# A product of constants ahead of the first weights, and the centring of W moved up, in a GNN and mixture-of-experts kernel on one core

## The chip, the cores and the metric

The kernel runs on one core of a Trainium2 chip. The metric is the device time of one execution in microseconds. The kernel before took 1074.32 us, the median of three runs (1073.18 to 1074.93).

## The reference

x has 6250 rows of 256 columns, and there are 206250 edges, sorted by their target (100000 drawn ones in both directions, and one loop for each node). The kernel computes, with LN for a layer norm without gain:

```
deg  = number of edges that end at a node (+1 for the second loop)
h    = LN(x) @ W;  norm = 1/sqrt(deg[src] * deg[dst])
agg  = segment_sum(h[src] * norm, dst) + b;  x = x + prelu(agg)
z    = LN(x);  routing = softmax(mean(z) @ Wr + br), rescaled, top 2 of 8 experts
ffn  = sum over the 2 experts of weight * (gelu(z @ W1 + b1) @ W2 + b2)
out  = x + LN(z + ffn) * gamma + beta
```

Two parts of it matter here. The layer norm in front of W is not applied to x: since LN subtracts the mean of each row, the kernel subtracts from each column of W that column's mean instead (it **centres** W), multiplies the raw x with it, and scales afterwards. And the degrees are found from the sorted targets.

## The kernel before

The 6250 nodes are T = 49 blocks of P = 128. Each engine runs its own program, and the order is written out by hand with semaphores. The stages are a prologue (until about 85 us), the sums over the edges (until about 764 us), the routing (until about 778 us) and the expert layers. Only the prologue is touched.

**SyncE** issues the loads in this order: the targets of all edges (`dst_all`, L576 and L578), W (L579), then x in five parts (L581).

**GpSimd** writes the first constants at L678: `ident`, `eps`, `ones` (128x128 of 1.0) and the first column of W. Each raises the semaphore `first_consts`; a fifth count comes from L680, which finishes `ident`. L682 then makes `position`, and further constants follow.

**TensorE** waits for all five counts and for W, and sums W's columns over the partitions with two f32 products, `ones` times W (L1708, into bank 5). Then `turn_x` (L1718) transposes the two halves of a block of x, two blocks ahead, and `make_h` (L1728) multiplies the turned block with W in two f32 products. `tiles(lo, hi)` is a `make_h` and a `turn_x` for each block. After `tiles(0, 5)` comes the flag product (L1743 and L1744, into bank 7), which says whether the degree search found a plain case; it waits for `unsorted_ready` and `found` from VectorE. `tiles(5, 7)` follow, then seven steps of twelve bf16 count products (L1753), one tile between two of them. L1780 is the first product that needs the degrees.

**VectorE** works in program order. L878 makes `rise`, the differences of neighbouring targets. L880 makes `mark[1]` from the targets and `position`: it is the second operation of the **degree search**. L884 centres W, in two operations, once TensorE's column sums are there (`w_mean`). L888 needs `rise` and `mark[1]`; then come L891, twelve maxima of 136 columns (L896), and small operations up to L913, which raises `unsorted_ready`. L917 reads the flag. Then VectorE makes the one-hot matrices of the counts (L936, L923, L940).

**ScalarE** copies every turned block out of PSUM (L1503) and every product (L1508), and sums its squares (L1516).

Of the kernel before, what the change touches and what calls it, by code (L numbers as in the profile page):

```python
# [6 lines left out]
ALU = mybir.AluOpType  # L7
# [9 lines left out]
P = 128  # L17
# [36 lines left out]
def edge_columns(E):  # L54

    assert RANGE % (2 * SC) == 0
    return -(-(-(-E // P)) // RANGE) * RANGE
# [7 lines left out]
def gnn_ffn_kernel(nc, a, out, E):  # L65
    x, src, dst, pairs = a["x"], a["src"], a["dst"], a["pairs"]
    N, D = out.shape
    NX, _, F = a["W1"].shape
    T = -(-N // P)
    REST = N - (T - 1) * P  # L70
    KD, KF = D // P, F // P
    COLS = edge_columns(E)
# [10 lines left out]
    POS_BITS = SEG.bit_length()  # L83
# [16 lines left out]
    WARM = (9, 8, 4)  # L100
    CF = TOP_K * KF
    GF = 4
    EARLY_W1 = 2
    GATHERED = sorted(d for first in GFIRST for d in range(first, T - 3, GCYCLE))
    FROM = 2
# [21 lines left out]
    HALVES = [(h * HALF, h * HALF + ROWS, list(picks(DENSE[h::2], GCYCLE - 1))) for h in range(2)]  # L127
    LISTED = list(picks(GATHERED, 1))
    N_KEYS = sum(len(cols) for _, _, cols in HALVES)
    N_STARTS = N_KEYS + len(LISTED)  # L130
    TABLE_PARTS = ((0, 8), (HELD, 32), (8, 16), (32, 40), (16, HELD), (40, T))
# [30 lines left out]
    with ExitStack() as ctx:  # L162
        def sb(name, shape, dt=F32):
            return ctx.enter_context(nc.sbuf_tensor(name, shape, dt))

        def sem(name):
            return ctx.enter_context(nc.semaphore(name))
# [10 lines left out]
        ones = sb("ones", [P, P])  # L178
# [67 lines left out]
        REGION_END = TAB_AT + T * 2 * D * WORD  # L246
        W1_AT = ADJ_AT - EARLY_W1 * KD * F * WORD
        assert (NX - EARLY_W1) * KD * F <= P * T and LAST == 1
        RING_AT = ADJ_AT - RING * (2 * D + P) * WORD - 2 * GCH * 2 * WORD - 64
# [50 lines left out]
        dst_all = room("dst_all", [P, COLS + 1], I32)  # L300
# [4 lines left out]
        position = room("position", [P, COLS])  # L305
        mark = [room(f"mark{i}", [P, COLS]) for i in range(2)]
# [30 lines left out]
        gl = room("gl", [P, 2, CF, GT * P], F32R)  # L337
        assert 2 * CF * GT * P >= (NX - EARLY_W1) * KD * F
        W2e = room("W2e", [P, TOP_K, KF, D])
# [4 lines left out]
        gh = room("gh", [P, 2, CF, GT * P], F32R)  # L344
        gf = room("gf", [P, GF, GT * P])
        zb, x1b = (room(n, [P, 2, GT, D]) for n in ("zb", "x1b"))
# [12 lines left out]
        cum_ps, off_ps, flag_ps = banks[5], banks[6], banks[7]  # L359
# [12 lines left out]
        position_made = sem("position_made")  # L372
# [5 lines left out]
        first_consts = sem("first_consts")  # L378
# [109 lines left out]
        N_FIRST = 5  # L488
# [58 lines left out]
        def block_edges(eng, d):  # L547

            return (eng.value_load(table[0:1, 0, ds(d, 1)], min_val=0, max_val=EDGES),
                    eng.value_load(table[0:1, 1, ds(d, 1)], min_val=1, max_val=MAXB),  # L550
                    eng.value_load(table[0:1, 2, ds(d, 1)], min_val=0, max_val=MAXB * T))
# [121 lines left out]
        def _(pool):  # L673
# [47 lines left out]
            def load_W1(lo, hi):  # L721
                for e in range(lo, hi):
                    g.dma_start(W1a[:, e, :, :], a["W1"][e, :, :].rearrange("(k p) f -> p k f", p=P)).then_inc(w1_in, 16)
# [5 lines left out]
            with pool.If(is_dense(pool)):  # L729
# [44 lines left out]
                pool.wait_ge(row_used, NGATH * GCH)  # L774
                load_W1(0, EARLY_W1)
                for d in (2 * GT - 2, 2 * GT - 1):
# [3 lines left out]
                pool.wait_ge(acc_ready, T - 1)  # L780
                load_W1(EARLY_W1, NX)
            with pool.Else():
                tab_made(pool)
                for buf, pattern, m in ((gpos, [[RANGE, NRANGE]], COLS), (block_node, [[P, T]], 0), (batch_starts, [[BATCH, MAXB]], 0)):
                    g.iota(buf[:, :], pattern, base=0, channel_multiplier=m, allow_small_or_imprecise_dtypes=True).then_inc(g_consts, 1)

                pool.wait_ge(table_ready, 1)
                pool.wait_ge(h_stored, 16)
                def gathers(d):
                    load_tile(d, 0)  # L790
                    _, n, first = block_edges(pool, d)
                    with pool.Fori(0, n) as j:
                        b = first + j
                        for h, (lo, hi) in enumerate(PARTS):
                            pool.wait_ge(src_in[h], (b + 1) * 16)
                            for u in range(lo, hi):
                                hold(pool, slot_free, b * U + (u + 1))
                                g.indirect_dma_start(
                                    out=rows[:, u, :], out_offset=None, in_=h_table,
                                    in_offset=bass.IndirectOffsetOnAxis(ap=src_ix[h][:, u - lo:u - lo + 1], axis=0),  # L800
                                    bounds_check=T * P - 1).then_inc(rows_in[u], 16)
                    store_x1(d, 0)
                    finish_x1(0, d * 16 + 16)

                with pool.Fori(0, T) as d:
                    gathers(d)
                pool.wait_ge(acc_ready, T)
                pool.wait_ge(x1_out, T + 2)
                load_W1(0, NX)
                load_x1()  # L810
# [31 lines left out]
        def _(dve):  # L842
            v = nc.vector
            pro = [0]

            def step(ins):
                pro[0] += 1
                ins.then_inc(dve_pro, 1)

            def settled():  # L850
                dve.wait_ge(dve_pro, pro[0])
# [5 lines left out]
            dve.sem_inc(zl_kept, KD)  # L857
            dve.sem_inc(gl_made, GF)
            dve.sem_inc(norm, 2 * NORM)
# [10 lines left out]
            def x_variance(tiles):  # L870
                settled()
                for t in tiles:
# [3 lines left out]

            dve.wait_ge(edges_in, 32)
            v.tensor_tensor(rise[:, :], dst_all[:, 1:COLS + 1], dst_all[:, 0:COLS], ALU.subtract).then_inc(rise_made, 1)  # L878
            dve.wait_ge(position_made, 1)
            step(v.scalar_tensor_tensor(out=mark[1][:, :], in0=dst_all[:, 0:COLS], scalar=float(1 << POS_BITS), in1=position[:, :],  # L880
                                        op0=ALU.mult, op1=ALU.add))
            dve.wait_ge(w_mean, 1)
            for k in range(KD):
                v.scalar_tensor_tensor(out=W[:, k, 1:D + 1], in0=cum_ps[:, 0:D], scalar=-1.0 / D, in1=W[:, k, 1:D + 1],  # L884
                                       op0=ALU.mult, op1=ALU.add).then_inc(w_centred, 1)
            dve.wait_ge(rise_made, 1)
            settled()
            step(v.scalar_tensor_tensor(out=mark[0][:, :], in0=rise[:, :], scalar=0.0, in1=mark[1][:, :], op0=ALU.is_gt, op1=ALU.mult))  # L888
# [87 lines left out]
            def root_of(lo, hi):  # L976
# [13 lines left out]
                                   op0=ALU.mult, op1=ALU.add).then_inc(decoded, 1)  # L990
# [404 lines left out]
            def split_g(g, k, n, tiles=range(CF)):  # L1395
                for c in tiles:
                    dve.wait_ge(g_made, g * (2 * CF) + (2 * c + 10))
                    v.tensor_tensor(gl[:, k, c, 0:n], gf[:, c % GF, 0:n], gh[:, k, c, 0:n].bitcast(F32), ALU.subtract).then_inc(gl_made, 1)  # L1398

# [58 lines left out]
            for k in range(TOP_K):  # L1458
# [4 lines left out]
                                         op0=ALU.mult, op1=ALU.add))  # L1463
            assert rs[0] == ROUTE_B2
            split_g(0, 0, GT * P, range(2, CF))
            for k in range(TOP_K):
                dve.wait_ge(w_split, 2 * TOP_K + k + 1)
                rstep(v.scalar_tensor_tensor(out=W2l[:, k, :, :], in0=W2e[:, k, :, :], scalar=wts[:, k:k + 1],
                                             in1=W2h[:, k, :, :].bitcast(F32), op0=ALU.mult, op1=ALU.subtract))
# [18 lines left out]
        def _(act):  # L1488
# [164 lines left out]
            def gelus(g, k, n, tiles):  # L1653
                for c in tiles:
# [5 lines left out]
                    act.wait_ge(gl_made, g * CF + (c + 1))  # L1660
                    s.activation(gf[:, c % GF, 0:n], h1_ps[c % 4][:, 0:n], ACT.Gelu, bias=bias).then_inc(g_made, 1)  # L1661

# [34 lines left out]
        def _(pe):  # L1697
            mm = nc.tensor.matmul
# [3 lines left out]
            pe.sem_inc(edges_turned, 1)  # L1702
            pe.sem_inc(z_turned, 2)
            pe.sem_inc(y_made, 2 * GT)
            pe.wait_ge(first_consts, N_FIRST)
            pe.wait_ge(w_in, 16)
            for q in range(KD):
# [40 lines left out]
            with pe.If(by_runs(pe)):  # L1748
                for c in range(RSTEPS):
                    k = c % 2  # L1750
                    pe.wait_ge(ones_ready, c * 2 + 2)
                    for q in range(SC):
                        last = mm(deg[:, 0:T], hot_src[:, k, :, q], hot_run[k][:, q // PAIR, :, q % PAIR],  # L1753
                                  start=(c == 0 and q == 0), stop=True, skip_group_check=True)
# [174 lines left out]
            with pe.Else():  # L1929
# [14 lines left out]
                with pe.Fori(0, T) as d:  # L1944
                    _, n, first = block_edges(pe, d)
# [41 lines left out]
            def output(g, k, n, between=None):  # L1987
                pe.wait_ge(rt, ROUTE_END)
                pe.wait_ge(gl_made, g * CF + (CF + GF))
                for m in range(n):  # L1990
# [70 lines left out]
```

## Time and profile before

| | us |
|---|---|
| median of three runs | 1074.32 |
| the profiled execution | 1075.31 |
| its span, first to last instruction | 1073.8 |
| outside the span | 1.5 |
| TensorE busy in the span | 1048.2 |
| VectorE busy | 815.8 |
| ScalarE busy | 683.0 |
| GpSimd busy | 518.9 |
| TensorE's first matmul starts | 6.5 |

Times are microseconds from the start of the span. A matmul's recorded length holds its way through the array as well as its columns, so matmuls that follow each other overlap in the records; how fast they go is read from the chain of work, which cuts them to what each adds. An f32 product is two passes, and has two matmul records and two weight loads. The granted clock of TensorE is a share of 2.4 GHz: 1.00 is the upper level, 0.50 the lower (1.2 GHz).

### The profile page before, as it was taken

What the parts mean: (1) busy time and instruction counts of PE and PEld (TensorE: products, weight loads), DVE (VectorE), ACT (ScalarE), POOL (GpSimd) and SP (SyncE); (2) the same over time, 40 slices, a digit from 0 to 9 for tenths busy, and PEclk for the clock granted to TensorE, in tenths of its full rate; (3) what the DMA queues carried; (4) which work ended last, traced back from release to release, by engine and by line L of the source; (5) the groups of instructions that cost most, each with busy time, mean ns of one, the idle gap of its engine ahead of it and who ended that gap; (6) DMA issues with size and microseconds to landing.
All of it is one profiled execution on the core that took longest, in us unless ns stands there. A gap on an engine that the chain in (4) does not pass through costs nothing.

```text
span 1073.8 us, 20081 instructions
## 1 busy us (share of the span) xinstructions
PE 1048.2 (98%) x6264; PEld 892.4 (83%) x6267; DVE 815.8 (76%) x1947; ACT 683.0 (64%) x1511; POOL 518.9 (48%) x520
## 2 busy tenths in 40 slices
PE   6999999999999999999999999999899999999996
PEld 5787888888888888888888888888689999999995
DVE  6897777868686867776777777866477878878786
ACT  5794565767666676666666766675386474656551
POOL 4102566677767776777677767771201111111111
PEclk9999999999999999999999999999899999999998
DMA  9067455566766676666667666664321111111101
GB/s 291 24 247 269 129 161 159 162 193 186 205 181 193 186 203 181 190 195 190 194 178 202 189 195 181 199 183 140 133 76 45 45 44 44 44 49 39 49 30 34
DMA packets 72547, 156.70 MB, mean 146 GB/s; under 512 B 11556, under 2 KB 38062, under 8 KB 72462
## 3 DMA queue, kind: packets, MB, share of 16 engines
q0 software_dynamic: 34896, 114.40, 37.0%
q1 hardware_dynamic: 37566, 41.22, 11.9%
q8 instruction: 46, 0.75, 0.3%
q14 instruction: 39, 0.32, 0.1%
HBM read 129.92 MB, written 25.67 MB: 145 GB/s over the span
## 4 chain that ended last, share of the span: by engine, by line
PE 92%; DVE 2%; ACT 2%; issue 1%; DMA 1%; ACTq 0%; SPq 0%; DVEq 0%; POOLq 0%; POOL 0%
PE banks L1869 40%; PE banks L1846 14%; PE banks L1983 11%; PE banks L1887 9%; PE banks L1996 8%; PE banks L1998 4%; PE banks L1728 3%; PE banks L1718 1%; PE banks L1823 1%; ACT gh L1659 1%; DMA xs<-in_x 1%; ACT gf L1661 1%; DVE hot_src L923 0%; PE banks L1857 0%; DVE hot_key L940 0%
## 5 line engine op out<-in xcount | busy, mean ns | idle before, releaser
L751 POOL DMA_INDIRECT row<-h_table,lists x385 | 436.0, 1133 | 215.8 <-issue 132.4
L1869 PE MATMUL banks<-tab,adj 128*128 128x512 f32 x1862 | 453.1, 393 | 1.3 <-ACT adj L1594 1.3
L1869 PEld LDWEIGHTS banks<-tab,adj 128*128 128x128 f32 x1862 | 348.0, 188 | 78.7 <-DVE tab L1044 1.4
L1589 ACT CAST adj<-banks 128x784 fp32r<-128x784 f32 x296 | 226.4, 817 | 216.5 <-PE banks L1846 216.5
L1156 DVE TENSOR_TENSOR hot_src<-iota_src,turned 128x1536 bf16<-128x1536 bf16 x152 | 146.3, 963 | 121.1 <-PE banks L1846 120.4
L1164 DVE TENSOR_TENSOR hot_key<-iota_key,turned 128x588 bf16<-128x588 bf16 (+1 forms) x456 | 199.5, 491 | 0.0
L1846 PEld LDWEIGHTS banks<-hot_key,hot_src 128*128 128x128 bf16 x1776 | 148.3, 145 | 39.3 <-issue 36.3
L1846 PE MATMUL banks<-hot_key,hot_src 128*128 128x147 bf16 (+1 forms) x1776 | 174.8, 247 | 0.6 <-ACT adj L1589 0.6
L1996 PE MATMUL banks<-W2s,gh 128*128 128x512 f32 x392 | 139.0, 396 | 0.6 <-DVE pre L1419 0.6
L1659 ACT ACTIVATE gh<-banks,b1e 128x384 fp32r<-128x384 f32 (+1 forms) x136 | 79.6, 585 | 87.3 <-PE banks L1983 87.2
L1606 ACT ACTIVATE hot_row<-iota,own_dst 128x128 fp32r<-128x128 f32 x385 | 127.2, 404 | 0.0
L1887 PE MATMUL banks<-row,hot_row 128*128 128x512 f32 x385 | 119.8, 421 | 0.0
L1998 PE MATMUL banks<-W2s,gl 128*128 128x256 f32 x392 | 109.5, 279 | 0.0
L1613 ACT ACTIVATE hot_row<-hot_row,ones 128x384 fp32r<-128x384 f32 (+3 forms) x154 | 83.7, 561 | 10.7
L1983 PE MATMUL banks<-zTh,W1h 128*128 128x384 f32 (+1 forms) x272 | 89.9, 332 | 0.4 <-ACT gf L1661 0.4
L1983 PE MATMUL banks<-zTl,W1h 128*128 128x384 f32 (+1 forms) x272 | 89.6, 331 | 0.0
L1996 PEld LDWEIGHTS banks<-W2s,gh 128*128 128x128 f32 x392 | 73.4, 187 | 16.1 <-DVE pre L1419 0.9
L1661 ACT ACTIVATE gf<-banks,b1e 128x384 f32<-128x384 f32 (+1 forms) x136 | 79.7, 586 | 6.5 <-DVE gl L1398 6.5
L815 POOL TENSOR_TENSOR rstdf<-vare,neg_half 128x1 f32 (+1 forms) x49 | 28.6, 583 | 114.0 <-DVE vare L1425 114.0
L1398 DVE TENSOR_TENSOR gl<-gf,gh 128x384 fp32r<-128x384 f32 (+1 forms) x136 | 66.7, 538 | 13.0 <-ACT gf L1661 12.6
L825 POOL DMA_DIRECT2D x1f<-x_dram x14 | 10.7, 764 | 131.7 <-DVE x1b L1408 122.3
L1998 PEld LDWEIGHTS banks<-W2s,gl 128*128 128x128 f32 x392 | 74.0, 189 | 0.0
(230 smaller groups left out, 1160.6 us busy)
## 6 DMA issues: line engine op xcount, KB each, us to landing
h_table<-tab SPq DMA_DIRECT2D x5, 2048.0 KB, 8.5
xin<-in_x SPq DMA_DIRECT2D x49, 128.0 KB, 4.2
x_dram<-x SPq DMA_DIRECT2D x49, 128.0 KB, 2.7
row<-h_table,lists POOLq DMA_INDIRECT x385, 3.8
x1f<-x_dram POOLq DMA_DIRECT2D x16, 384.0 KB, 3.8
out<-res SPq DMA_DIRECT2D x48, 128.0 KB, 1.7
W1a<-in_W POOLq DMA_DIRECT2D x8, 512.0 KB, 6.0
xs<-in_x SPq DMA_DIRECT2D x2, 1536.0 KB, 14.8
```

Source lines behind the costliest of these rows:

```text
L751: g.indirect_dma_start(out=row[:, u, :].bitcast(F32), out_offset=None, in_=h_table, in_offset=bass.IndirectOffsetOnAxis(ap=lists[:, m % 2, ...
L1156: v.tensor_tensor(hot_src[:, kk, :, :].rearrange("p n (j c) -> p n j c", j=CPG), iota_src[:, :, :].rearrange("p n (j c) -> p n j c", j=CPG ...
L1164: v.tensor_tensor(hot_win[s % 2][j], iota_key[:, lo:hi, :].rearrange("p (o n) c -> p o n c", o=1).to_broadcast(shape), rows_turned(b, 1)[: ...
L1589: s.copy(adj[k][:, :].rearrange("p (q n) -> p q n", n=P)[:, :, at:at + 2 * GN].rearrange("p q (b n) -> p q b n", b=2), bank_pairs[j][:, :, ...
L1606: s.activation(hot_row[:, u, :], iota[:, :], ACT.Square, bias=own_dst[:, c:c + 1]).then_inc(squared, 1)
L1661: s.activation(gf[:, c % GF, 0:n], h1_ps[c % 4][:, 0:n], ACT.Gelu, bias=bias).then_inc(g_made, 1)
L1846: last = mm(adj_ps[g][:, lo:hi], hot_src[:, kk, :, j * SG + g], hot_win[kk][j][:, g // PAIR, :, g % PAIR], start=(j == 0), stop=True, skip ...
L1869: last = mm(acc[k][:, :], adj[k][:, q * P:(q + 1) * P], tab[:, q, :], start=(at == 0), stop=(at == T - 1), skip_group_check=True)
L1887: mm(acc_row[:, :], hot_row[:, n % RING, :], row[:, n % RING, :], start=(j == 0), stop=False, skip_group_check=True).then_inc(row_used, 1)
L1983: last = mm(h1_ps[c % 4][:, 0:n], w[:, e, q, f * P:(f + 1) * P], z[:, k, q, 0:n], start=(i == 0), stop=(i == len(terms) - 1))
L1996: mm(y[:, 0:2 * D], gh[:, k, c, m * P:(m + 1) * P], W2s[:, c // KF, c % KF, :, :].rearrange("p h d -> p (h d)"), start=(c == 0), stop=Fals ...
L1998: last = mm(y[:, 0:D], gl[:, k, c, m * P:(m + 1) * P], W2h[:, c // KF, c % KF, :], start=False, stop=(c == CF - 1), skip_group_check=True)
```

## The change

Two edits in the prologue.

TensorE, as soon as four of the five first constants are there, multiplies `ones` with itself 24 times (f32, 128 columns, into bank 7, results unused), and only then waits for the fifth constant and for W.

VectorE centres W directly after L878, ahead of L880. Nothing else is moved.

```diff
     WARM = (9, 8, 4)
     CF = TOP_K * KF
     GF = 4
+    WARM_UP = 24
@@ VectorE
             v.tensor_tensor(rise[:, :], dst_all[:, 1:COLS + 1], dst_all[:, 0:COLS], ALU.subtract).then_inc(rise_made, 1)
-            dve.wait_ge(position_made, 1)
-            step(v.scalar_tensor_tensor(out=mark[1][:, :], in0=dst_all[:, 0:COLS], scalar=float(1 << POS_BITS), in1=position[:, :],
-                                        op0=ALU.mult, op1=ALU.add))
             dve.wait_ge(w_mean, 1)
             for k in range(KD):
                 v.scalar_tensor_tensor(out=W[:, k, 1:D + 1], in0=cum_ps[:, 0:D], scalar=-1.0 / D, in1=W[:, k, 1:D + 1],
                                        op0=ALU.mult, op1=ALU.add).then_inc(w_centred, 1)
+            dve.wait_ge(position_made, 1)
+            step(v.scalar_tensor_tensor(out=mark[1][:, :], in0=dst_all[:, 0:COLS], scalar=float(1 << POS_BITS), in1=position[:, :],
+                                        op0=ALU.mult, op1=ALU.add))
             dve.wait_ge(rise_made, 1)
@@ TensorE
             pe.sem_inc(y_made, 2 * GT)
+            pe.wait_ge(first_consts, N_FIRST - 1)
+            for _ in range(WARM_UP):
+                mm(flag_ps[:, 0:P], ones[:, :], ones[:, :], start=True, stop=True)
             pe.wait_ge(first_consts, N_FIRST)
             pe.wait_ge(w_in, 16)
```

## Rows read from the trace of the kernel before

**Rows 1.** The page: busy us by engine, and the granted clock in 40 slices.

```profile
PE 1048.2 (98%) x6264; PEld 892.4 (83%) x6267; DVE 815.8 (76%) x1947; ACT 683.0 (64%) x1511; POOL 518.9 (48%) x520
PEclk9999999999999999999999999999899999999998
```

**Rows 2.** Chain that ended last, 0 to 95 us: start, us it adds, work.

```profile
2.53 6.91 DMA xs<-in_x
...
9.49 1.11 PE banks L1718 x4
...
10.73 2.05 PE banks L1728 x4
12.78 0.43 PE banks L1718 x2
13.21 1.71 PE banks L1728 x4
...
15.35 1.01 PE banks L1728 x4
...
17.67 0.87 PE banks L1728 x4
18.55 0.22 PE banks L1718 x2
18.76 0.12 PE banks L1743 x2
...
20.30 0.47 DVE hot_key L936
...
34.83 0.21 DVE deg_sb L972
...
35.40 0.36 PE banks L1780 x2
```

**Rows 3.** Timeline, 0 to 45 us, VectorE's search: start, us, operation.

```profile
7.62 1.85 DVE L880 SCALAR_TENSOR_TENSOR mark<-dst_all,position 128x1632 f32<-128x1632 int32 x1
...
9.39 0.75 DVE L884 SCALAR_TENSOR_TENSOR W<-banks,W 128x256 f32<-128x256 f32 x2
...
10.05 1.85 DVE L888 SCALAR_TENSOR_TENSOR mark<-rise,mark 128x1632 f32<-128x1632 f32 x1
...
11.94 0.20 DVE L891 COPY mark<-mark 128x12 f32<-128x12 f32 x1
...
16.27 0.14 DVE L913 TENSOR_SCALAR unsorted<-fall 128x1 f32<-128x1 f32 x1
```

**Rows 4.** The same timeline: first constants, and VectorE's and TensorE's first work.

```profile
1.53 0.10 POOL L678 MEMSET W<- 128x2 f32 x1
...
1.88 0.28 POOL L680 TENSOR_SCALAR_AFFINE_SELECT ident<-ident 128x128 f32<-128x128 f32 x1 [0.24 <-POOL W L678]
...
5.85 1.86 DVE L878 TENSOR_TENSOR rise<-dst_all 128x1632 f32<-128x1632 int32 x1 [5.73 <-DMA dst_all<-in_dst]
...
6.51 2.04 PE L1708 MATMUL banks<-W,ones 128*128 128x256 f32 x4 [6.51 <-DMA W<-in_W]
```

**Rows 5.** The chain again: twelve f32 passes of 49 columns.

```profile
37.72 1.31 PE banks L1785 x12
```

**Rows 6.** Half-microsecond stretches (us, busy by engine, PEclk, DMA), and TensorE's timeline.

```profile
776.50:777.00 0.50, 0.50 (x5) 0.50 (x4) 0.15 (x1) 0.50 (x2) 0.36 (x1) 0.81 0.00 0
...
1064.00:1064.50 0.50, 0.34 (x2) 0.03 (x1) 0.50 (x2) 0.00 (x0) 0.16 (x1) 1.00 0.00 0
...
1066.50:1067.00 0.50, 0.00 (x0) 0.00 (x0) 0.47 (x2) 0.00 (x0) 0.00 (x0) 0.82 0.63 217
...
772.02 0.25 PE L1799 MATMUL banks<-Wr,zmean 128*1 128x8 f32 x4 [2.80 <-DVE zmean L1349]
```

**Rows 7.** Who waited for whom, 0 to 36 us: total us, times, longest.

```profile
PE banks L1780 <- DVE deg_loop L974: 1.1, 1, 1.1
...
PE banks L1753 <- DVE hot_key L940: 0.8, 1, 0.8
```

## Prediction

> **What bounds the kernel now.** I read the page's busy line first, then the chain of work that ended last, then the timeline of the first 20 us, then the granted clock in half microseconds. TensorE is busy for 1048.2 of 1073.8 us [rows 1], so in nearly all of the kernel a microsecond that the start gains or loses is still there at the end. The change touches only the first 20 us, so the question is which chain ends last there.
>
> The chain of the first 36 us has three pieces [rows 2]. It is DMA until 9.45, when the first part of x has landed. Then it is TensorE alone, from the first transposes at 9.49 through tiles 0 to 4 to the flag product of L1743 at 18.76. Then it is VectorE: the flag, the one-hot compares from 20.30 on, the degrees. At 35.40 TensorE takes over again (L1780) and keeps the chain. Whatever moves the flag product moves everything behind it.
>
> VectorE is not in the first 19 us of the chain, but it runs close beside it [rows 3]. L880 starts at 7.62, the two centring operations at 9.39, L888 at 10.05, L891 at 11.94; the search ends with L913 at 16.27 + 0.14 = 16.41. L1743 needs both that end and the end of tile 4. So VectorE has 18.7 - 16.4 = 2.3 us to spare, and no more.
>
> TensorE's early tiles are slow. Four passes of 257 columns take 1.71 us at 13.21 and 0.87 at 17.67; two transposes take 0.43 and 0.22 [rows 2]. That is 0.213 us for 128 f32 columns, later 0.107: the lower level of the clock (1.2 GHz), later the upper (2.4 GHz). The page's PEclk shows full clock there too [rows 1]; I go by the durations. The four passes at 15.35 took 1.01 us, between the two: 0.28 us of them at the low rate, so the rise was near 15.6. At the low rate tiles 0 to 4 took 8.0 us (10.73 to 18.76 [rows 2]); at the upper rate they are 5 x (0.87 + 0.22) = 5.45. The warm-up is after these 2.6 us.
>
> **The change, step by step.** *When the warm-up starts.* It waits for the fourth constant, the W memset, which ends at 1.63; GpSimd's own wait for the same count ended at 1.88 [rows 4]. I take 1.8.
>
> *How much work it is.* Each f32 product is two passes, since L1708's two products are four matmul records [rows 4]. So 24 products are 48 passes of 128 columns. At 0.107 us that is 5.12 us, at 0.213 us 10.24 us. No row shows this very form back to back. The transposes have the same columns and the same f32 weight load of 128 columns, and run at 0.107 with the load hidden; I take them. The dearer bound is L1785: twelve passes of 49 columns in 1.31 us, 0.109 each [rows 5], where the columns alone are 0.041. If the other 0.068 were added to every pass, a pass would be 0.175 and the 48 passes 8.4 us at the upper clock.
>
> The Trainium skill, "TensorE: Matmul & The Clock Gate", section "Back-to-back issue gap", speaks against the cheap value: in a stream of load and matmul pairs it gives some 81 ns for 128 columns where a lone matmul needs 56. As an estimate by that page, 25 ns on each of 48 passes would end the warm-up 1.2 us later. No row here shows this pair.
>
> *When the clock rises.* Two rises can be timed. In the routing stage TensorE took up work at 772.02 and the mean clock of 776.50 to 777.00 is 0.81, so the rise was at 776.69, 4.7 us later [rows 6]. In the prologue it came 6.1 us after the transposes of 9.49, with small gaps on the way. The warm-up has no gaps, so I take 4.7 and keep 6.1 as a bound; nothing shows that it can't be sooner, so I keep at once (0) as the other.
>
> *When the warm-up ends.* Until the rise the passes run at half rate: end = 1.8 + 5.12 + half the time to the rise. That is 9.3 (4.7 us), 10.0 (6.1 us), 6.9 (at once) and 12.0 (never). W landed and was in use at 6.51 [rows 4]. So 24 products are too many: the column sums of W (L1708), which ran from 6.51 to 8.55, now start at 9.3.
>
> *What waits for that.* At the upper clock the sums take 4 x 0.213 = 0.85 us, and about 0.2 us pass until VectorE starts, so centring starts at 9.3 + 1.07 = 10.35. Here the second edit counts. Before, L880 (1.85 us) ran while W's sums were being made. Now VectorE finishes L878 at 7.71 [rows 4] and stands 2.6 us before the centring, with L880, L888 and the whole search queued behind it. From the starts in [rows 3]: centring to the operation behind it 0.66, L880 to L888 1.89 (as from L888 to L891), L888 to the end of L913 6.36, and 0.12 to reach TensorE, 9.03 together. So the flag product comes at the warm-up's end + 1.07 + 9.03 = + 10.1, which is 19.4. Against 18.7 in the profile that is 0.7 us later.
>
> *What the warm-up buys.* W is centred at 10.35 + 0.75 = 11.1 against 10.14, and the x copies are there before that. Five tiles at the upper clock end at 11.1 + 5.45 = 16.6. TensorE gains 2.1 us and then waits 2.8 us for the search. The gain is real but off the chain: the search is late next. Break-even is a warm-up that ends at 18.7 - 10.1 = 8.6.
>
> *Other effects at nothing.* The warm-up writes bank 7, which nobody uses before L1743, and the edit issues no DMA, so no queue moves. ScalarE starts its tiles about 0.4 us later and has the 2.8 us as cover. GpSimd is untouched.
>
> *The reference.* Added to the profiled execution (1075.31, span 1073.8 and 1.5 around it) 0.7 gives 1076.0. The runs' median is 1074.32, 1.0 lower. A part of that can be the late rise: had it come 4.7 us after 9.49, at 14.2 instead of 15.6, tiles 0 to 4 would have ended (15.6 - 14.2)/2 = 0.7 earlier, and the other runs may have had that. The changed kernel has no such gain. So against the median I expect between 0.7 and 1.4 more and take 1.2: **1075.5**.
>
> **The rivals.**
>
> *A. The clock falls in the new gap.* At the end of the kernel TensorE's last matmul ends at 1064.34, and the clock falls at 1066.82 (mean 0.82 in that half microsecond), after 2.5 us without work [rows 6]. The gap that I expect is 2.8 us. If the clock falls there, tiles 5 and 6 and the first counts run at half rate until the next rise. A rise after 4.7 us costs 2.35 us of TensorE's time. TensorE had 0.8 us to spare before the first count [rows 7] and about 0.5 of the 1.1 before L1780, since VectorE itself reached L972 only at 34.83 [rows 2]. About 1.0 us is left: 1076.5. For it: gap and time to fall are nearly equal. Against: the fall need not come in the gap at all. The section "HAM oscillation" of the same page describes such a return to the low clock in waits between bursts of matmuls; the end of this trace agrees.
>
> *B. The warm-up ends before it can hurt: the faster side.* If the clock rises almost at once, the warm-up ends at 6.9, the search passes the flag product at 6.9 + 10.1 = 17.0, and TensorE's tiles are done by then: x still lands at 9.45, so tile 0 starts at about 10.4 and five tiles end at 15.9. That is 1.7 us earlier than in the profile, some 1.1 against the median: 1073.2. It decides from a warm-up end below 8.6. Against it: in both rises of the trace the clock took 4.7 us or more.
>
> *C. The weight loads aren't hidden.* With 0.175 us a pass the warm-up ends at 1.8 + 8.4 + 2.35 = 12.6 and the flag product comes at 22.7, 4.0 late: 1078.8. For it the rate of L1785; against it the transposes.
>
> *D. The change doesn't do what it says:* this product doesn't raise the clock. The warm-up ends at 12.0, the sums of W take 1.0 more, the flag product comes at 23.1: 4.4 late, 1079.2 or more. Against it: both kinds of matmul in the trace were followed by a rise.
>
> **How the numbers follow.** A change of 0.2% is 2.15 us, which is about what a measurement of this kernel can tell from none. Forecast (search late, clock stays up) 0.48; A 0.27; B 0.12; C 0.09; D 0.04. The forecast's own spread is 1074.6 to 1076.2. Only the far end of B is faster by 0.2%: 0.03. Slower by 0.2% are C, D and the part of A with a late rise, 0.13 + 0.08 = 0.21. The rest, 0.76, is the same. The range takes in the forecast, A and B: 1073.3 to 1077.0; it leaves out C and D and a little of A.
>
> **What would show it.** In the changed profile: 48 matmul records of the warm-up from about 1.8 on, ending near 9.3, the early ones at twice the pitch of the late ones; L1708 starting at its end and not at 6.5; VectorE idle 2.6 us before L884; L880 behind it; tiles 0 to 4 in about 5.5 us, ending near 16.6; TensorE idle some 2.8 us before L1743, released by VectorE's L913; L1743 at 19.4. From there to L1780 16.6 us as before; if that is more and tiles 5 and 6 take twice as long, A is right. I am wrong if the warm-up ends before 8.6, or if L1743 isn't released by VectorE.

## The result, and the profile after

The changed kernel takes 1077.41 us, the median of eight runs (1075.97 to 1079.77); the kernel before 1074.29, the median of eight (1073.18 to 1075.65). The ratio is 1.0029, with a 95% interval of 1.0019 to 1.0039. That is 3.1 us slower, 0.29% (the lower end of the interval is 0.19%, beside the 0.2% of my forecast), and 0.4 us above my range.

The ratios in this document go by all executions of a series, not by the two medians alone, and can differ by 0.1% or a little more from the quotient of the medians.

The profiled execution took 1075.97 us with a span of 1074.5. It is the fastest of the eight and 1.4 us below their median. Its busy line:

```profile
PE 1051.8 (98%) x6312; PEld 898.0 (84%) x6315; DVE 815.8 (76%) x1947; ACT 683.1 (64%) x1511; POOL 521.4 (49%) x520
```

TensorE has 48 matmuls more and 3.6 busy us more than in [rows 1]: the products start at 2.05, and until 6.51 TensorE had nothing to do. Line numbers are four higher on TensorE: L1708 is now the warm-up, and the column sums of W are L1712. On VectorE they are one higher, but for the two pieces that changed places: the centring L884 is now L882, and L880 is L885. The timeline of the changed kernel's start, with start, length, operation and idle time in front:

```profile
2.05 7.14 PE L1708 MATMUL banks<-ones 128*128 128x128 f32 x48 [2.05 <-POOL W L679]
...
9.02 1.03 PE L1712 MATMUL banks<-W,ones 128*128 128x256 f32 x4
...
10.09 0.76 DVE L882 SCALAR_TENSOR_TENSOR W<-banks,W 128x256 f32<-128x256 f32 x2 [2.38 <-PE banks L1712]
...
10.77 1.85 DVE L885 SCALAR_TENSOR_TENSOR mark<-dst_all,position 128x1632 f32<-128x1632 int32 x1
...
12.72 1.86 DVE L889 SCALAR_TENSOR_TENSOR mark<-rise,mark 128x1632 f32<-128x1632 f32 x1
...
18.95 0.14 DVE L914 TENSOR_SCALAR unsorted<-fall 128x1 f32<-128x1 f32 x1
...
19.14 0.19 PE L1747 MATMUL banks<-ones,unsorted 128*1 128x1 f32 x2 [2.53 <-DVE unsorted L914]
```

The column sums of W start at 9.02, where they started at 6.51 [rows 4]. VectorE idles 2.38 us in front of the centring, and L885, which ran at 7.62 as L880 [rows 3], now starts at 10.77. TensorE has finished tile 4 and then idles 2.53 us until L914. The flag product comes at 19.14 instead of 18.69 (its start in the timeline of before; the chain of [rows 2] cuts it to 18.76).

The chain behind it (start, what it adds, work), and TensorE's granted clock (the figure third from the end; before it busy time by engine, behind it DMA):

```profile
19.14 0.19 PE banks L1747 x2
19.33 0.05 PE banks L1748 x2
19.38 2.01 PE banks L1732 x4
21.39 0.43 PE banks L1722 x2
21.82 1.20 PE banks L1732 x4
...
23.95 0.96 PE banks L1732 x4
...
36.16 0.36 PE banks L1784 x2
```

```profile
18.00:19.00 1.00, 0.00 (x0) 0.00 (x0) 0.93 (x8) 0.00 (x0) 0.00 (x0) 0.97 1.09 347
19.00:20.00 1.00, 0.86 (x6) 0.73 (x7) 0.24 (x3) 0.00 (x0) 0.00 (x0) 0.50 1.10 350
...
22.00:23.00 1.00, 1.00 (x6) 0.81 (x5) 1.00 (x4) 0.73 (x3) 0.00 (x0) 0.82 1.09 347
```

So the clock fell to its lower level at 18.94, inside TensorE's wait, and rose at 22.36. Tile 5 took 2.01 us and tile 6 1.20 where a tile takes 0.87 to 0.96. L1784, the first product that needs the degrees, comes at 36.16, 0.76 us after the 35.40 of [rows 2], and the span is 0.7 us longer. The first product after the flag, tile 5, is in these rows L1732 at 19.38, tile 6 L1732 at 21.82.

That leaves a question: this trace explains 0.7 us and the medians differ by 3.1.

### The profile page after: what moved, and what is told of

The parts are those of the page before. It is cut to its first block, busy times and chain, and to the rows that moved or that the text cites. A ratio compares the mean times of both kernels' runs of the same rounds, so it can differ in the third digit from the quotient of the medians.

```text
span 1074.5 us, 20177 instructions
## 1 busy us (share of the span) xinstructions
PE 1051.8 (98%) x6312; PEld 898.0 (84%) x6315; DVE 815.8 (76%) x1947; ACT 683.1 (64%) x1511; POOL 521.4 (49%) x520
## 3 DMA queue, kind: packets, MB, share of 16 engines
q0 software_dynamic: 34896, 114.40, 37.3%
## 4 chain that ended last, share of the span: by engine, by line
PE 94%; ACT 2%; DVE 2%; issue 1%; ACTq 0%; POOL 0%; POOLq 0%; DVEq 0%; PEldq 0%
PE banks L1873 40%; PE banks L1850 14%; PE banks L1987 11%; PE banks L1891 9%; PE banks L2000 8%; PE banks L2002 4%; PE banks L1732 4%; PE banks L1827 1%; PE banks L1722 1%; ACT gh L1660 1%; PE banks L1708 1%; ACT gf L1662 1%; PE banks L1757 0%; PE banks L1861 0%; PE banks L1893 0%
```

## The experiments

I call **S** the theory that the degree search now stands behind the warm-up and W's sums, with the fall of the clock as a consequence. Rivals: **W** (a letter only, not the matrix), the products cost the time by themselves; **O**, the new order does; **R**, the rest is lost in another stage. Each experiment's trace gave the numbers of this table. Times are starts in us; "sums" is the first operation that needs W, "degrees" is L1780 of the kernel before or the line that answers to it, "behind" is the span less that time.

| kernel | sums | flag product | degrees | flag to degrees | behind | ratio to before, 95% interval |
|---|---|---|---|---|---|---|
| before, trace 1 | 6.51 | 18.69 | 35.40 | 16.71 | 1038.4 | |
| before, trace 2 (e6) | 7.12 | 16.36 | 33.07 | 16.71 | 1038.5 | 0.9996 (0.9987 to 1.0005) |
| changed, trace 1 | 9.02 | 19.14 | 36.16 | 17.02 | 1038.3 | 1.0029 (1.0019 to 1.0039) |
| changed, trace 2 (e1) | 9.25 | 19.43 | 36.50 | 17.07 | other chip | 1.0028 (0.9994 to 1.0062) |
| changed, trace 3 (e5) | 9.05 | 19.17 | 36.15 | 16.98 | 1038.7 | 1.0027 (1.0017 to 1.0037) |
| changed, trace 4 (e12) | 9.66 | 19.79 | 36.92 | 17.13 | 1038.4 | 1.0020 (1.0011 to 1.0030) |
| changed, gap filled (e7) | 10.22 | 20.34 | 36.95 | 16.61 | 1038.9 | 1.0025 (1.0016 to 1.0034) |
| 24 products, old order (e2) | 9.30 | 17.47 | 34.09 | 16.62 | other chip | 0.9980 (0.9947 to 1.0013) |
| 24 products, old order (e9) | 10.14 | 18.34 | 34.94 | 16.60 | 1038.6 | 0.9996 (0.9987 to 1.0005) |
| new order alone (e3) | 6.57 | 17.72 | 34.47 | 16.75 | other chip | 1.0020 (0.9988 to 1.0051) |
| new order alone (e10) | 6.60 | 17.74 | 34.44 | 16.70 | 1038.5 | 1.0005 (0.9995 to 1.0014) |
| 12 products, new order (e4) | 6.81 | 17.22 | 33.94 | 16.72 | other chip | 1.0006 (0.9977 to 1.0036) |
| 12 products, new order (e11) | 6.75 | 17.21 | 33.90 | 16.69 | 1038.6 | 0.9998 (0.9989 to 1.0007) |
| 12 products, old order (e8) | 7.19 | 16.45 | 33.16 | 16.71 | 1038.5 | 0.9995 (0.9986 to 1.0004) |

e1 to e4 shared a chip on which every kernel, the one before too, took about 1114 us and spread from 1106 to 1126. Their ratios say nothing at this size; their first 36 us are like those of the other chips and are used. I repeated the four where that mattered.

**The changed kernel again (e1_again).**

> The changed kernel once more, for a second trace of it. Theory S (the degree search stands behind the warm-up and W's sums, and the clock falls while TensorE waits for it): L1747, the flag product, at 19.1 us again and L1784 at about 36.2, and a median near 1077.4; whatever the median has beyond the 0.8 us of the first trace shows in the first 36 us as a longer stretch at the low clock (L1784 at 37 to 38). Rival R (the rest is lost in another stage): L1784 at 36.2 in this trace too, and a difference of 1 to 2 us after it, most likely in the routing stage between 764 and 778 us, where the clock falls as well.

Flag product at 19.43, degrees at 36.50: as S had it, and not yet an answer to R.

**Each edit alone.** 24 products with the old order; this edit and the ones below are shown without the lines around them:

```diff
+    WARM_UP = 24
...
+            pe.wait_ge(first_consts, N_FIRST - 1)
+            for _ in range(WARM_UP):
+                mm(flag_ps[:, 0:P], ones[:, :], ones[:, :], start=True, stop=True)
             pe.wait_ge(first_consts, N_FIRST)
```

> 24 products, but the centring of W stays behind the second operation of the degree search. Theory S: W's sums still end near 10.1, yet VectorE uses its wait: L888 of the kernel before starts near 10.75 and not 12.7, the flag product comes at 17.3 (19.1 with both edits, 18.7 before), TensorE waits only 0.6 us for it, the clock stays up there, and L1780 of the kernel before comes 1.4 us sooner than before, near 34.0: 1072.9, range 1072.3 to 1074.0. Rival W (the warm-up alone costs the time, whatever stands behind it): flag product at 19.1 and the median near 1077.

> 24 products, old order on VectorE, once more, hoping for less spread than in the first series (1108 to 1118). Theory S, with the start at 2.05 and the pitch of 0.112 us that the traces showed: warm-up ends between 9.0 and 10.7 by the clock's rise, the flag product 8.1 us later (17.1 to 18.8, first trace 17.47), the clock stays up, L1784 at 33.7 to 35.4; against the kernel before, whose flag product lies between 16.4 and 18.7, no difference: ratio 0.9990 to 1.0005. Rival W (the products cost the 3 us by themselves): ratio 1.0025 or more.

In e9 the sums of W are later than in any trace of the changed kernel (10.14), and still the flag product comes at 18.34:

```profile
7.63 1.85 DVE L881 SCALAR_TENSOR_TENSOR mark<-dst_all,position 128x1632 f32<-128x1632 int32 x1
...
11.21 0.76 DVE L885 SCALAR_TENSOR_TENSOR W<-banks,W 128x256 f32<-128x256 f32 x2 [1.74 <-PE banks L1712]
11.89 1.89 DVE L889 SCALAR_TENSOR_TENSOR mark<-rise,mark 128x1632 f32<-128x1632 f32 x1
...
18.34 0.19 PE L1747 MATMUL banks<-ones,unsorted 128*1 128x1 f32 x2 [0.60 <-DVE unsorted L914]
```

L881 runs in VectorE's wait, so that L889 follows the centring at once, 0.7 us after its start; in the changed kernel that distance is 12.72 - 10.09 = 2.63. The ratio is 0.9996. W falls: 24 products cost nothing that can be measured as long as the search isn't behind them. They gain nothing either.

The new order alone is the changed kernel less these lines:

```diff
-            pe.wait_ge(first_consts, N_FIRST - 1)
-            for _ in range(WARM_UP):
-                mm(flag_ps[:, 0:P], ones[:, :], ones[:, :], start=True, stop=True)
```

> No products, only the centring moved up. Theory S: W's sums end at 8.55 as before, L880 moves behind the centring and the search ends near 17.5, still ahead of tile 4's end at 18.7, so nothing changes: 1074.3, range 1073.7 to 1075.0. Rival O (the new order costs by itself, about as much as the 1.1 us by which the search ends later): flag product at 19.8, 1075.4.

> No products, centring moved up, once more. Theory S: the search ends at 17.5 at the soonest (first trace: flag product 17.72), so the executions with an early rise of the clock lose 1.1 us against the kernel before (16.36 there) and those with a late rise nothing: flag product 17.6 to 18.8, ratio 1.0002 to 1.0010. Rival O (the order is what costs the 3 us): ratio 1.0025 or more.

The flag product comes at 17.72 and 17.74, released by VectorE in both, and the ratio is 1.0005: O falls as the cause of 3 us.

```profile
17.74 0.19 PE L1744 MATMUL banks<-ones,unsorted 128*1 128x1 f32 x2 [2.18 <-DVE unsorted L914]
```

In e3 I had expected tile 4 to be the last (18.7). It wasn't, since the clock had risen early in both traces; that was the first sign of what follows.

**The same kernel in other executions.** e5_after_third and e12_after_fourth are the changed kernel, e6_before_again the kernel before, all without an edit.

> The changed kernel, a third trace. In the first two the warm-up ended at 9.2 and 9.4, the flag product came at 19.14 and 19.43, and L1784 at 36.16 and 36.50. Theory S: what varies between executions is when the clock rises after the warm-up's start (3.2 and 3.7 us so far); each microsecond of it moves the warm-up's end and the flag product by half, and moves the fall and the next rise of the clock with it, so that the flag product lies between 19.1 and 20.7 and L1784 between 36.1 and 37.6. Rival R (another stage): L1784 at 36.2 to 36.5 again while the whole is still 2 us and more over the kernel before.

> The kernel before once more, for a second trace. In the first the clock rose at 15.6, which is late, and the flag product came at 18.7 and L1780 at 35.40. Theory S: with an earlier rise TensorE's tiles end sooner, down to the search's own end at 16.4: flag product between 16.5 and 18.9, L1780 between 33.1 and 35.5, so that the first trace of the kernel before was one of its late ones. Rival R: flag product and L1780 where they were.

> The changed kernel, a fourth trace. Three traces had an early rise (warm-up ended at 9.19, 9.38 and 9.19), while the kernel with the filled gap had a late one (10.36). Theory S: a trace with a late rise shows the flag product near 20.3 and L1784 near 37.3 and a span near 1076; one with an early rise shows 19.2, 36.2 and 1074.7 again. Ratio to before 1.0020 to 1.0035. Rival R: the span differs from 1074.7 by over 1 us while L1784 stays at 36.2.

e6 is the kernel before, and its chain reads quite differently from [rows 2] and [rows 3]:

```profile
7.58 1.77 DVE mark L880
...
10.02 1.78 DVE mark L888
...
16.24 0.07 DVE unsorted L913
16.32 0.04 issue
16.36 0.19 PE banks L1743 x2
```

The search is on the chain and the tiles are not: from 10.15 on they ran at the upper clock. The flag product comes at 16.36, 2.3 us sooner than in trace 1, and so do the degrees (33.07) and the end (span 1071.6, 1073.07 us).

e12 is the changed kernel with a later rise in the warm-up:

```profile
2.05 7.78 PE banks L1708 x48
...
19.79 0.19 PE banks L1747 x2
19.98 0.05 PE banks L1748 x2
20.02 1.73 PE banks L1732 x4
21.75 0.43 PE banks L1722 x2
22.18 1.68 PE banks L1732 x4
...
36.92 0.36 PE banks L1784 x2
```

It took 1076.73 us, just the median of its series. The column "behind" answers R: over ten traces on the chips with little spread, the time from the degrees to the end is 1038.3 to 1038.9 us, whatever the kernel. In these executions all that the change moved lies in the first 36 us, and R falls for them. It isn't excluded for executions without a trace. In traces 1 and 3 of the changed kernel the traced execution was the fastest of its series (1075.97 and 1076.26, medians 1077.41 and 1077.23), and of the executions of this kernel above 1077 us on these chips none was traced.

**Filling the gap (e7_fill_gap).**

```diff
             tiles(0, 5)
+            for _ in range(10):
+                mm(flag_ps[:, 0:P], ones[:, :], ones[:, :], start=True, stop=True)
             pe.wait_ge(unsorted_ready, 1)
```

> The changed kernel, and after tile 4 ten more products of the constant with itself (2.2 us at the upper clock), in the 2.5 us in which TensorE waits for the search. Theory S with rival A of the forecast (the clock falls in that gap): granted clock 1.00 from 16 to 24 us, the flag product where it was (19.1 to 20.7), and from there to L1784 16.7 us, as in the kernel before, in place of 17.0 to 17.6; 0.3 to 1.0 us faster than the changed kernel. If the fall costs nothing: the same distance as in the changed kernel.

```profile
17.65 2.40 PE L1746 MATMUL banks<-ones 128*128 128x128 f32 x20
20.34 0.19 PE L1749 MATMUL banks<-ones,unsorted 128*1 128x1 f32 x2 [0.29 <-DVE unsorted L914]
```

```profile
18.00:20.00 2.00, 2.00 (x19) 1.86 (x17) 1.86 (x13) 0.78 (x4) 0.00 (x0) 1.00 1.09 348
20.00:22.00 2.00, 1.71 (x13) 1.45 (x13) 0.49 (x5) 0.32 (x2) 0.00 (x0) 1.00 1.09 350
22.00:24.00 2.00, 1.25 (x11) 0.88 (x10) 2.00 (x5) 1.92 (x8) 0.00 (x0) 1.00 1.09 345
```

The clock stays up, and flag to degrees is 16.61 us against 16.98 to 17.13 in the four traces with the fall. The fall costs 0.4 to 0.5 us. The traces with the old order (e2, e8, e9), in which the clock didn't fall either, have 16.60 to 16.71. In the runs the cost is not resolved: the median is 0.65 below e5's (1076.58 against 1077.23), the intervals of the ratios overlap.

**Fewer products.** `WARM_UP = 12`, with the new and the old order.

> Both edits with 12 products in place of 24. Theory S: the warm-up ends near 6.4, W's sums run at 6.5 as soon as W is there and at the upper clock, the search is the limit with its end at 16.7, the tiles end near 15.9, and the flag product comes at 16.8, 1.9 us sooner than before: 1072.4, range 1071.8 to 1073.8. Rival W (products cost by themselves): half of the loss of 3.1 us stays, 1075.9. Rival C (12 products don't raise the clock early enough, or it falls again between 7.5 and 9.5 while x is awaited): tiles 0 to 4 at half rate for a part, flag product near 18, 1074.

> Both edits with 12 products, once more. Theory S: W's sums start at 6.5 to 7.2, the search ends 8.97 us after VectorE starts to centre, flag product 16.9 to 17.8 (first trace 17.22), L1784 33.6 to 34.6: ratio 0.9993 to 1.0005. Against the changed kernel 2.5 us less, which is what the second dozen of products costs when the search stands behind it. Rival: ratio 1.001 to 1.0015, half the loss.

> 12 products, and the centring of W behind L880 as before. Theory S: the warm-up ends at 6 to 7, W's sums are done by 8.2, VectorE's search runs exactly as in the kernel before (L888 of it at 10.05) and ends at 16.4, TensorE's tiles end near 16, the flag product comes at 16.6 and L1780 at 33.3: 2.1 us sooner than in the first trace of the kernel before and about 1.3 sooner than its mean. Both edits with 12 products gave 17.22 and 33.94. Rival C (the clock falls while x is awaited): tiles at half rate, flag product at 18 or later.

With 12 products the sums of W come at 6.75 to 7.19, about when W is there. Flag product 17.21 and 17.22 with the new order, 16.45 with the old one, in which the search itself is undisturbed. I expected 16.8 in e4: the sums started at 6.81 and not 6.5, and L885 took 2.13 us instead of 1.85, see below. Against the changed kernel e11 is 2.6 us faster in the same series (1074.10 against 1076.73), and e8 is 3.7 faster (1073.48 against 1077.23). Against the kernel before neither differs beyond its interval (0.9998 and 0.9995); I had expected e4 to gain 1.9 us on it and e8 1.3. No version beats the kernel before beyond its interval: the best that a warm-up can do is to bring the tiles below the search, and in executions like e6 they are there already. The spread of e8 is worth a look all the same. Ten of its eleven executions took 1073.22 to 1073.75 us and one 1076.35, where only 10 of the 31 of the kernel before on that chip, and 6 of e6's 11, took 1073.75 or less; the medians are 1073.48 and 1074.61. That 12 products with the old order hold the kernel at its fast end would fit S, but no run was made to show it.

## Why the prediction was wrong

**Right.** The chain and the order of events: the warm-up ends near 9.2 and not before 8.6; the sums of W (L1712) wait for it; VectorE idles 2.4 us (I said 2.6) in front of the centring with the search queued behind; the tiles end at 16.6 (16.6); TensorE waits 2.53 us (2.8) and is released by L914; flag product at 19.14 (19.4). From the sums' start to the flag product it is 10.12 to 10.18 us in the four traces of the changed kernel; I had 10.1. Rivals B, C and D did not come.

For the traced execution I had 1076.0 and it took 1075.97. That is in part luck: the flag product came 0.3 us sooner than forecast, and the fall of the clock, which the forecast left out, added 0.4 behind it.

**Wrong: the last step, from the traced execution to the median.** I said "against the median I expect between 0.7 and 1.4 more and take 1.2", so 0.5 us less than in the trace; the median is 1.4 us more than the trace. Three terms of the sum were too small.

*The reference.* The profiled execution of before was one of its late ones: 1075.31, where the median is 1074.3 and e6 took 1073.07. I let only 0.5 of this 1.0 us count, and credited the other executions with 0.7 us at most, from a rise of the clock 4.7 us after 9.49. In e6 the tiles ran at the upper clock from 10.15, and the flag product fell to the end of the search, 16.36. The 2.3 us of spare time on VectorE that I computed was therefore also the size of what the kernel before can gain in a good execution, and I did not use it so. The change takes this gain away: its search ends at 19.1 at the soonest seen. This term was 0.5 us short.

*The fall of the clock, put at nothing.* I kept it out of the sum as rival A, with a chance of 0.27. It came in all four traces of the changed kernel, and by my own test (more than 16.6 us behind the flag product, tiles 5 and 6 slow) A is what happened. I priced it at 1.0 us; it cost 0.4 to 0.5 at the degrees. In trace 1, tiles 5 and 6 with their transposes took 2.01 + 0.43 + 1.20 + 0.22 = 3.9 us, where two tiles at the upper clock take 2.2 [rows 2]; of these 1.7 us about 1.3 were absorbed by TensorE's spare time ahead of the degrees, as I had counted, but I had put the loss at 2.35 us. The low clock lasted 3.4 us and not 4.7.

*The warm-up's end.* The start was 2.05, not 1.8 (GpSimd's last memset reached TensorE 0.4 us after its end). The pitch was 0.112 us and not 0.107: the 20 passes of e7 take 2.40 us with one pass's own length of 0.27, (2.40 - 0.27) / 19. Together these are 0.5 us. And the rise varies. With 48 x 0.112 = 5.38 us of work, the sums' start less 2.05 less 5.38 is about half the time at the low rate, which makes the rise 3.2 us after the start in traces 1 and 3, 3.7 in e1, 3.8 in e2, 4.5 in e12, 5.4 in e9 and 5.6 in e7. So the sums started between 9.02 and 10.22, in the middle trace at 9.30, which is my 9.3: in traces 1 and 3 an early rise made up for the other two. The runs say that the typical warm-up ended later. If nothing else varies between the executions of a series, the median lies as far from the traced one as its sums do: 9.7 in e12's series, 9.5 in e7's, 9.8 in e9's, but 10.0 in e5's and 10.5 in the first. This is an estimate from the times, and the last of these is later than any sums that a trace shows.

Of the 1.9 us by which the median missed my 1075.5, the reference is 0.5, and the fall 0.4 to 0.5. About 1.0 is left for a warm-up that ends near 10.3 in place of 9.3. A rise at 5.6 us as in e7 (flag product 20.34) and the fall's 17.0 behind it would give degrees at 37.3, and the medians of 1077.2 and 1077.4 need 37.3 and 37.5; but no trace of the changed kernel itself shows it. So the share of this third term stays open, as does the reason why the clock's rise is early in one execution and late in the next.

**The page on the clock.** "Back-to-back issue gap" of the Trainium skill's "TensorE: Matmul & The Clock Gate" had led me to an estimate of 25 ns more for each of the 48 passes. Measured, a pass is 0.112 us, 5 ns above the transposes' 0.107: the time of the load is nearly all hidden. The page's figure for the lone matmul is measured on bf16, and for the 81 ns it names no type; here the products are f32.

## What to carry to other kernels

Before pulling work in front of a queue, ask what the queue did in the time that it now spends waiting: here the two edits cost nothing each (0.9996 and 1.0005) and 2 to 3 us together, because the moved wait was harmless only as long as it ended early. Size a warm-up by the wait that it fills and not by the clock that it wants, and give the time gained on one engine a place to go. And when two chains run 2 us apart and one of them depends on the clock, one trace is one draw: read a second before taking the profiled time as the reference.

## What the hardware showed that I had not expected

In all four traces of the changed kernel TensorE waited 2.53 to 2.59 us for the search, and the clock fell near the end of that wait or up to 0.5 us behind it: at 18.94, 18.99, 19.43 and 20.28. Each time it stayed low for 3.4 us. In e12 that is 20.28 to 23.69:

```profile
20.00:20.50 0.50, 0.50 (x3) 0.47 (x3) 0.15 (x1) 0.00 (x0) 0.00 (x0) 0.78 1.10 352
20.50:21.00 0.50, 0.50 (x2) 0.41 (x2) 0.00 (x0) 0.00 (x0) 0.00 (x0) 0.50 1.08 344
...
23.50:24.00 0.50, 0.50 (x5) 0.31 (x4) 0.50 (x1) 0.10 (x1) 0.00 (x0) 0.81 1.23 374
```

There it fell after TensorE had resumed at 19.79, so a gap of this length is paid for behind its end. In e3, e4, e10 and e11 TensorE waited 1.74 to 2.18 us in the same place, and the granted clock stayed at 1.00. During the first microseconds of every trace the granted clock reads 1.00 while products take twice their time; there only the durations tell the level.

Some operations of VectorE and GpSimd take longer side by side. With 12 products and the new order L885 lies beside GpSimd's L695:

```profile
8.56 2.11 DVE L885 SCALAR_TENSOR_TENSOR mark<-dst_all,position 128x1632 f32<-128x1632 int32 x1
```

```profile
8.93 1.87 POOL L695 TENSOR_SCALAR_AFFINE_SELECT order<-order 112x112 bf16<-112x112 bf16 x1
```

In trace 1 of the changed kernel L695 takes 0.27 us and L885 1.85. In the same way L692 takes 1.36 us in the kernel before, where L880 runs beside it, and 0.49 as L693 of the changed kernel, where VectorE is idle; L880 isn't slowed by it (1.85). So GpSimd wasn't untouched, as the prediction had it, though nothing on the chain came of that. In e11 GpSimd's operation ends 0.13 us after VectorE's. That they wait for one another is a reading of these rows and was not tested.
